# When the weights of layer 1 are made: one group in each of supertiles 2 to 7 of layer 0, and the copies of the last three groups on GpSimd

## The reference, cut to what matters

```python
# layer 0, slope 0.01, h = x; layer 1, slope 0.2, h = x @ W
e = (h @ a1)[:, None] + (h @ a2)[None, :]
e = leaky_relu(e, slope)
e = where(adj > 0, e, -9e15)
y = softmax(e, axis=1) @ h          # layer 1: elu(y)
x = layernorm(x + y, axis=-1)
```

## Time and profile before

| | |
|---|---|
| median of 3 runs | 428.86 us (428.27 to 428.87) |
| profiled execution, its time | 428.54 us |
| its span (first to last instruction) | 426.9 us |
| TensorE matmul busy | 397.4 us, 93% |
| ScalarE busy | 382.8 us, 90% |
| VectorE busy | 365.1 us, 86% |
| GpSimd busy | 270.0 us, 63% |
| granted TensorE clock, mean | 0.989 |

### The profile page before, as it was taken

The page is one execution under the profiler, slowest core; times in us unless marked ns, Lnnn a source line. Parts: engine busy times, 40 slices in busy tenths (PEclk is TensorE's granted clock), DMA queues, the critical chain, the costliest instruction groups (busy, mean ns, idle before and its releaser), DMA issues.

```text
span 426.9 us, 11669 instructions
## 1 busy us (share of the span) xinstructions
PE 397.4 (93%) x4372; PEld 386.2 (90%) x4372; DVE 365.1 (86%) x687; ACT 382.8 (90%) x603; POOL 270.0 (63%) x323
## 2 busy tenths in 40 slices
PE   3789999999999999999989989999999999999980
PEld 1478898999999999999989989999999999999980
DVE  4799999899889888888988978798998989898863
ACT  3889994998989899998989989999999999999920
POOL 4744297493976959597681227576757667584941
PEclk9999999999999999999999999999999999999995
DMA  5999959989999899999800000000000000000000
GB/s 119 97 104 104 90 44 93 98 60 107 72 101 103 68 102 69 107 78 88 73 14 2 14 14 2 2 26 2 27 2 26 2 25 0 25 0 25 2 26 16
DMA packets 38844, 21.66 MB, mean 51 GB/s; under 512 B 1808, under 2 KB 38800, under 8 KB 38800
## 3 DMA queue, kind: packets, MB, share of 16 engines
q0 software_dynamic: 33792, 16.78, 50.5%
q1 hardware_dynamic: 3920, 3.25, 2.5%
q10 hardware_dynamic: 1088, 1.05, 0.7%
HBM read 69.30 MB, written 2.10 MB: 167 GB/s over the span
## 4 chain that ended last, share of the span: by engine, by line
PE 51%; DVE 14%; ACT 14%; issue 11%; POOL 7%; DMA 1%; DVEq 0%; POOLq 0%; ACTq 0%
PE acc L1268 47%; ACT neg L688 13%; DVE neg L865 3%; DVE split L851 2%; DVE pos L877 2%; PE tb L1184 2%; DMA x_chunks<-in_x 1%; PE srcb L1205 1%; DVE mask_t L949 1%; DVE packs L771 1%; POOL scr L378 1%; DVE mask_t L779 1%; POOL scr L359 1%; POOL scr L357 1%; DVE dcol L957 1%
## 5 line engine op out<-in xcount | busy, mean ns | idle before, releaser
L1268 PE MATMUL acc<-wmov,pos 128*128 128x195 bf16 x2016 | 356.3, 248 | 7.8 <-DVE pos L877 7.4
L688 ACT ACTIVATE neg<-srcb,dcol 128x512 int8<-128x512 f32 x512 | 357.0, 1073 | 0.0
L1268 PE MATMUL acc<-wmov,neg 128*128 128x195 bf16 x2016 | 356.3, 249 | 0.0
L1268 PEld LDWEIGHTS acc<-wmov,pos 128*128 128x128 fp8e5 x2016 | 198.6, 98 | 13.0 <-DVE pos L877 11.3
L1268 PEld LDWEIGHTS acc<-wmov,neg 128*128 128x128 fp8e5 x2016 | 197.6, 98 | 1.4 <-issue 0.7
L877 DVE SCALAR_TENSOR_TENSOR pos<-mask_t,neg 128x512 uint32<-128x512 uint32 x128 | 104.2, 814 | 13.1
L865 DVE SCALAR_TENSOR_TENSOR neg<-mask_t,neg 128x512 uint32<-128x512 uint32 x128 | 100.6, 786 | 15.7 <-ACT neg L688 14.3
L495 POOL DMA_DIRECT2D enc<-in_adj x64 | 49.2, 772 | 12.8 <-DMA x_chunks<-in_x 4.5
L357 POOL TENSOR_TENSOR scr<-scr,acol 128x260 f32<-128x260 f32 x14 | 13.3, 948 | 56.5 <-issue 46.6
L893 DVE TENSOR_REDUCE scr<-acc 128x130 f32<-128x390 f32 x60 | 31.6, 558 | 4.1 <-PE acc L1268 2.6
L340 POOL TENSOR_TENSOR split<-val,bcol 128x520 f32<-128x520 f32 x15 | 16.5, 1100 | 20.0 <-DVE scr L404 10.3
(11 more groups left out here) (139 smaller groups left out, 311.4 us busy)
## 6 DMA issues: line engine op xcount, KB each, us to landing
enc<-in_adj POOLq DMA_DIRECT2D x64, 256.0 KB, 11.2
x_chunks<-in_x ACTq DMA_DIRECT2D x4, 256.0 KB, 5.6
x_rows<-xout SPq DMA_DIRECT2D x8, 128.0 KB, 5.5
resid<-x_rows SPq DMA_DIRECT2D x8, 128.0 KB, 2.1
out<-xout SPq DMA_DIRECT2D x8, 128.0 KB, 1.7
resid<-in_a SPq DMA_DIRECT2D x1, 64.0 KB, 4.5
resid<-in_w SPq DMA_DIRECT2D x2, 16.0 KB, 5.0
att<-in_a SPq DMA_DIRECT2D x2, 0.2 KB, 5.3
```

The lines of the kernel that those rows point to most:

```text
L688: ins = nc.scalar.activation(neg[:, k % SR, :, b], srcb[:, q % 2, :], ACT.Sign, bias=dcol[:, layer, c:c + 1])
L1268: ins = nc.tensor.matmul(acc[t][:, side * WC:(side + 1) * WC], m[:, t * P:(t + 1) * P, b], wmov[:, layer, c, side * WC:(side + 1) * WC], s ...
```

## The change

Group g (0 to 5) now goes through its whole chain in supertile g + 2 of layer 0: centred in step 1 (group 0 in step 4), exponentials in step 3 (group 0 in step 5), multiplied on GpSimd in step 5, after the end of the epilogue and between the third and the fourth load, weighed in step 7, after the extract. ScalarE copies the parts of groups 0 to 4 in step 1 of the next supertile. The copies of groups 5, 6 and 7 are on GpSimd (`keep_late`), in supertile 0 of layer 1; the multiply of group 7 waits for the GpSimd copy of group 5, and TensorE's steps 5, 6 and 7 of that supertile wait for those copies.

```diff
--- before.py
+++ after.py
@@ -37,6 +37,7 @@
 FEWER = 4
 WEIGH = 2
 XP = 4
+LATE = 5
 MEAN_STEPS = (2, 4)
 SUMS = 0
 
@@ -336,7 +337,10 @@
 
             if n > 1:
                 eng.wait_ge(w_vec, WEIGH * (n - 1))
-                eng.wait_ge(w_act, n - 1)
+                if layer == 1 and i - 2 >= LATE:
+                    eng.wait_ge(w_pool, i - 1 - LATE)
+                else:
+                    eng.wait_ge(w_act, n - 1)
             ops.tensor_tensor(parts_of(i)[:, :, :, 0, :], val[:, cs, :].unsqueeze(2).broadcast_to([P, NB, 2, FD]),
                               bcol[:, :, cs].rearrange("p s b -> p b s").unsqueeze(3).broadcast_to([P, NB, 2, FD]),
                               ALU.mult).then_inc(w_prod, 1)
@@ -531,35 +535,44 @@
                 loads = {0: (0,), 3: (1,), 5: (2,), 6: (3,)} if layer == 0 and not (is_first(q) or is_last(q)) else {}
 
                 groups = {}
-                if layer == 0 and not (is_first(q) or is_second(q) or is_third(q)):
-                    groups = {2: (q - 3,), 5: (q - 2,)} if is_last(q) else {2: (q - 3,)}
+                if layer == 0 and not (is_first(q) or is_second(q)):
+                    groups = {5: (q - 2,)}
                 for k in range(KB):
                     if k < 5:
                         for u in loads.get(k, ()):
                             load_adj(q + 1, u)
                     if done is not None and k in stages:
                         stages[k](pool, nc.gpsimd, *done)
-                    if k >= 5:
+                    if k == 5:
                         for u in loads.get(k, ()):
                             load_adj(q + 1, u)
                     for g in groups.get(k, ()):
                         multiply(pool, nc.gpsimd, 1, g)
+                    if k > 5:
+                        for u in loads.get(k, ()):
+                            load_adj(q + 1, u)
                     if layer == 0 and k == 6 and q >= 2:
                         add_values(q - 2)
 
             def change_layers():
 
 
+                keep_late(5)
                 add_values(NQ - 2)
                 pool.wait_ge(pdone[0], EPI[0] * NQ - 4)
                 multiply(pool, nc.gpsimd, 1, 6)
                 pool.wait_ge(pdone[0], EPI[0] * NQ - 3)
                 nc.gpsimd.tensor_tensor(rstd, var, mhalf, ALU.pow).then_inc(pdone[0], 1)
 
-                w = weights_of(1, 7).rearrange("p b (s c) -> p b s c", s=2)[:, :, :, 0:2 * FD]
-                pool.wait_ge(w_vec, WEIGH * (NQ + 7) + 1)
-                nc.gpsimd.tensor_copy(w, top_of(7).rearrange("p b s r c -> p b s (r c)")).then_inc(w_pool, 1)
+                keep_late(6)
                 add_values(NQ - 1)
+                keep_late(7)
+
+            def keep_late(i):
+
+                w = weights_of(1, i).rearrange("p b (s c) -> p b s c", s=2)[:, :, :, 0:2 * FD]
+                pool.wait_ge(w_vec, WEIGH * (NQ + i) + 1)
+                nc.gpsimd.tensor_copy(w, top_of(i).rearrange("p b s r c -> p b s (r c)")).then_inc(w_pool, 1)
 
             def add_values(g):
 
@@ -712,21 +725,16 @@
                     if layer == 0 and is_second(q) and k == KB - 1:
                         exps_of_s(0, 2, NQ)
 
-                    if layer == 0 and not (is_first(q) or is_second(q) or is_last(q)):
-                        if k == 6:
+                    if layer == 0 and not (is_first(q) or is_second(q)):
+                        if k == (5 if is_third(q) else 3):
                             exps_of_group(q - 2, is_odd(q))
-                    if layer == 0 and is_last(q):
-                        if k == 4:
-                            exps_of_group(q - 2, 1)
-                        if k == 5:
+                        if k == 1 and not is_third(q):
                             keep_parts(1, q - 3)
                     if layer == 1 and is_first(q):
                         if k == 0:
                             group_values(NQ - 2)
                         if k == 2:
                             exps_of_group(NQ - 2, 0)
-                        if k in (0, 6):
-                            keep_parts(1, {0: 5, 6: 6}[k])
                     if layer == 1 and is_second(q) and k == 1:
                         exps_of_s(1, 0, NQ)
 
@@ -734,8 +742,6 @@
                         group_values(q - 2)
                     if layer == 0 and done is not None and k == KB - 1:
                         copy_turned(done[1])
-                        if not (is_second(q) or is_third(q) or is_last(q)):
-                            keep_parts(1, q - 3)
                     if done is not None and done[0] == 1 and k == 5:
                         elu(done[1])
 
@@ -1095,14 +1101,12 @@
                         if k == 3:
                             take_max(1)
                     if layer == 0 and not (is_first(q) or is_second(q)):
-                        if k == (1 if is_last(q) else 4):
+                        if k == (4 if is_third(q) else 1):
 
                             dve.wait_ge(grp_set, 3 * (q - 1))
                             apart(dve, q)
                             centre_group(q - 2)
-                        if k == (4 if is_last(q) else 6) and not is_third(q):
-                            weigh(1, q - 3)
-                        if k == 6 and is_last(q):
+                        if k == 7:
                             weigh(1, q - 2)
 
             def finish():
@@ -1249,8 +1253,8 @@
                 if is_first(q):
 
                     pe.wait_ge(w_vec, WEIGH * (NQ * layer + k + 1))
-                    if layer == 1 and k == KB - 1:
-                        pe.wait_ge(w_pool, 1)
+                    if layer == 1 and k >= LATE:
+                        pe.wait_ge(w_pool, k - LATE + 1)
                     else:
                         pe.wait_ge(w_act, NQ * layer + k + 1)
                 for t in range(TI):
```

## The result

The changed kernel takes 429.38 us (median of 20 runs, 428.86 to 430.58), the kernel before 428.72 us (20 runs on the same chips). The ratio is 1.0017, with a 95% interval of 1.0012 to 1.0023: 0.66 us slower. The profiled execution took 429.49 us with a span of 427.9.

What follows compares the result with a forecast made beforehand. TensorE was taken to set the pace in full supertiles, its gaps elsewhere being all there was to win. Terms -1.52 + 1.56 - 0.42 + 0.31 gave -0.07 us, 428.8 us against the median, range 427.2 to 430.3.

Steps and rivals of the forecast that it cites:

- part 3: GpSimd's multiply moves from step 2 to step 5: nobody is kept waiting by it, cost 0.
- part 2: Supertile boundaries of layer 0: the weigh, now behind step 7's extract, lengthens VectorE's chain, a loss of 1.56 us in all.
- part 4: Supertile 0 of layer 1: ScalarE loses two copies and its waits for the weigh, TensorE's step 4 comes sooner, -0.42 us.
- Part 1: Supertile 7 of layer 0: group 4's weigh leaves step 4, so TensorE's step 5 is no longer late, -1.52 us.
- part 5: Supertile 0 of layer 1: GpSimd's copy of group 6 and value sums beside VectorE's masks delay step 7, +0.31 us.
- Rival B: Layer 0 boundaries: GpSimd's loads and value sums beside VectorE lengthen the chain, sum +1.1 us, 430.0 us; chance 0.19.
- Rival A: Supertile 0 of layer 1: GpSimd's copy and value sums wait, not the masks; sum -1.18 us, 427.7 us; chance 0.24.
- Rival C: Layer 0 boundaries cost nothing because VectorE lets the weigh in early; sum -2.0 us, 426.9 us; chance 0.07.

Runs made afterwards that it cites:

- e9: Kernel before, supertile 7's weighs in steps 6 and 7, group 4's copy in step 0 of layer 1, group 5's on GpSimd, group 6's on ScalarE: 426.23 us.
- e2: Changed kernel with the GpSimd multiply of group 0 (supertile 2) cut to one block of four: 428.22 us, ratio to the kernel before 0.9988.
- e1: Changed kernel with the weigh of step 7 ahead of the extract instead of behind it: 428.57 us, ratio to the kernel before 0.9996.
- e4: Changed kernel with the weigh in step 6, behind the pack, instead of step 7: 428.71 us, ratio to the kernel before 1.0002.
- e5: Changed kernel with the GpSimd multiply of groups 1 to 5 back in step 2: 429.54 us, ratio to the kernel before 1.0023.
- e6: Changed kernel with the multiply of groups 1 to 5 in step 2 and the weigh ahead of the extract: 427.28 us, ratio 0.9967.
- e11: Kernel before with only the copy of group 5 moved from ScalarE to GpSimd: 427.87 us, ratio 0.9985.
- e3: Changed kernel with group 6's copy on ScalarE and group 7's copy ahead of the last value sums: 428.06 us, ratio to the kernel before 0.9990.
- e7: Changed kernel, weigh ahead of the extract, multiply of groups 1 to 5 in step 2, of group 0 in step 7, group 6's copy on ScalarE: 426.97 us.
- e8: Kernel before with only the GpSimd multiply moved from step 2 to step 5 in supertiles 3 to 6: 432.50 us, ratio 1.0091.

## Why the prediction was wrong, point by point

The step that failed is part 3: the move of the multiply was priced at 0, and it cost 0.90. The other errors nearly cancel each other, the one of part 2 at 0.28 too little loss and the one of part 4 at 0.38 too little gain, so it is partly luck that the time came within the range.

**Part 1 (-1.52) held.** K5 of supertile 7 follows K4 by 3.22 in place of 4.73: -1.51. e9 gets the same (3.22) by two steps' shift.

**Part 2 (+1.56) named the right chain and fell short at one boundary.** Measured from supertile 2 to K4 of supertile 7: +0.54, +0.56, +0.66, +0.17, +0.50, +0.31, together 2.74. Supertiles 4 to 7 were forecast 0.48, 0.10, 0.48 and 0.3. Two things were missed. The larger is in supertiles 2 and 3, 1.10 where I took 0.2 between 0 and 0.48: e2 shows 0.90 of it to be the multiply, which belongs to part 3, and leaves the 0.2. The smaller is 0.15 at K0 of supertile 5 (2.92 after K7, where 2.77 is usual). TensorE's step 0 waits for VectorE's sums of the tile that it is to overwrite, a wait that I had not listed. The first sum starts at 155.41 and holds VectorE some 0.5 us, and K0 came at 156.12; this boundary alone crosses the end of the loop of two, and `negative` starts 0.2 later there. That the loop's end is the reason is argued, not tested.

**Part 3 (0) is the step that failed.** I priced the move of the multiply by its queue and its waiters, and took for cover that nobody waits for it. I did not ask which VectorE instructions it would newly lie beside, although part 5 of the same forecast does just that for the copy. In step 2 it ran beside the statistics, as the kernel before shows in supertile 5, with no `negative` held up behind it:

```profile
164.45 0.61 DVE L907 BATCH_NORM_STATS2 bst<-scr 128x6 f32<-128x64 f32 x4 [0.71 <-POOL scr L404]
165.16 0.38 DVE L911 BATCH_NORM_AGGREGATE mv<-bst 128x2 f32<-128x6 f32 x4
165.45 0.67 DVE L865 SCALAR_TENSOR_TENSOR neg<-mask_t,neg 128x512 uint32<-128x512 uint32 x1
...
164.37 1.07 POOL L340 TENSOR_TENSOR split<-val,bcol 128x520 f32<-128x520 f32 x1
```

In step 5 it runs beside masks. In supertiles 4 to 6 that cost was there but hidden under part 2 (e1 and e4 leave 25.3, e5 leaves 25.5, e6 25.0). In supertile 2, where the looks leave VectorE no time, it came out: 0.90 (0.54 in supertile 2, 0.36 at the start of supertile 3). This alone is more than the distance between -0.07 and the measured +0.66.

**Part 4 (-0.42) was too small.** K4 comes 11.50 after K0 and waits for nothing: -0.80. I counted the two waits of 0.21 that the rows name and took the rest of VectorE's time as work; e11 shows that all of the stall was ScalarE's copy of group 5. Waits too short to be printed are part of a busy-looking stretch.

**Part 5 (+0.31) held.** K7 comes 10.77 after K4 (10.57 before): +0.20, and the next K0 0.06 later. Without the copy and the value sums beside the masks it is 9.74 (e3). `negative` is 0.86 too long, where I took 0.87.

**The sum again:** -1.51 + 2.74 - 0.80 + 0.26 = +0.69, against the 0.66 of the medians. Rival B had the right sign and the right kind of cause (GpSimd's work beside VectorE's), but the wrong instructions and the wrong steps: it added up the loads and value sums of steps 6, 7 and 0 over five boundaries, and the one that counted was the multiply beside `negative` of step 6 in supertile 2. Rival A is out: `negative` waited for the copy in both places. Rival C is out, since the extract rules until the weigh is put ahead of it.

## What to carry to other kernels

When a GpSimd instruction is moved, ask not only who waits for it but which VectorE instructions with two operands in SBUF it will run beside, and price it there at nearly its whole remaining length. Here it cost nothing beside the statistics. Where a full stretch has two chains of nearly equal length, undoing one shows only the difference: try them singly and together before a cause is weighed. And a stall in one step calls for moving that step's work by a step or two, not the whole order by a supertile.

## What the runs showed of the hardware

A VectorE instruction of line 865 or 871 (`negative`), 883 (`positive`) or 777 (pack) that starts while GpSimd runs a multiply or a copy ends 0.54 to 0.55 us after that one's end. Five pairs show it: `negative` with the multiply of group 0 (it took 1.41 us), with the copy of group 6 (1.54) and with the copy of group 7 in the kernel before (0.92), `positive` with the multiply in e1 (1.37), the pack with the multiply in e7 (1.55). Alone each takes 0.68 to 0.69. By the rule of exclusive use in the Trainium skill (SBUF — State Buffer, section Who interferes with whom) the later one waits whole; the traces agree, but for 0.14 us: the wait is that much shorter than what was left of the GpSimd instruction.

What I had not expected: in e1 the first of the two slow masks, from 197.03 to 198.35, began 1.1 us before the multiply's start in the profile (198.16), while GpSimd issued loads, and it too was 0.6 too long. The order of the starts does not explain it. Loads alone do not hold a mask up. In e6, where the multiply is elsewhere, both masks of step 6 (supertile 5 here) lie beside four of them and take 0.69 each:

```profile
171.77 0.69 DVE L871 SCALAR_TENSOR_TENSOR neg<-mask_t,neg 128x512 uint32<-128x512 uint32 x1
172.57 0.69 DVE L883 SCALAR_TENSOR_TENSOR pos<-mask_t,neg 128x512 uint32<-128x512 uint32 x1
...
171.62 3.05 POOL L499 DMA_DIRECT2D enc<-in_adj  x4
```

Nor does it take the multiply: in e7 `negative` of step 6 in supertile 2 took 1.52 us from 95.81, beside loads and then the value sums (from 96.77). What holds these up stays open; the profile calls spans on GpSimd rough.

Moving one 1.1 us instruction of an engine that is busy 63% of the span by three steps cost 4.0 us (e8), since its delay passed from GpSimd over VectorE and ScalarE back to VectorE in each of four supertiles.
